# Attention inner loop: the two heads' score matmuls issued apart, with head a's value matmuls between them

## What is computed

```python
def reference(...):
    xn = _layernorm(x)
    x = x + attn(xn) + ffn(xn)
    return x

# attn
Q = rope((x @ Wq.T + bq) as 32 heads of 64)
K = rope((x @ Wk.T + bk) as 8 heads of 64), repeated 4 times
V = (x @ Wv.T + bv) as 8 heads of 64, repeated 4 times
scores = einsum('bhqd,bhkd->bhqk', Q, K) / sqrt(64)
attn = einsum('bhqk,bhkd->bhqd', softmax(scores), V)
out = attn @ Wo.T + bo

# ffn
gated = silu(x @ w_gate.T) * (x @ w_up.T)      # hidden 8192
out = gated @ w_down.T
```

## Time and profile before

| what | value |
|---|---|
| median of the 3 runs shown | 4861.9 us |
| the 3 runs | 4738.34, 4861.9, 4987.0 us |
| the profiled execution | 4735.85 us |
| its span, slowest core (core 1) | 4734.3 us |
| spans of the 8 cores | 4723.9 to 4734.3 us |
| busy: TensorE, ScalarE, VectorE | 3513.7, 1321.4, 902.3 us |

### The profile page before, as it was taken

How to read it: one execution, slowest core, us unless ns; L and a number is a source line. 1 busy time by engine, 2 the same in 40 slices (tenths; PEclk the granted TensorE clock), 3 DMA queues, 4 the chain that set the end, 5 groups by cost and what they waited for, 6 DMA issues and landing times.

```text
span 4734.3 us, 36748 instructions; the slowest of 8 cores (4723.9 to 4734.3 us)
## 1 busy us (share of the span) xinstructions
PE 3513.7 (74%) x13898; PEld 1223.7 (26%) x13898; DVE 902.3 (19%) x1009; ACT 1321.4 (28%) x1612; POOL 224.2 (5%) x428
## 2 busy tenths in 40 slices
PE   3656555555777777777777777749998995999899
PEld 0212111111211111111111111114444442444344
DVE  3242333333011111111111111130000002000000
ACT  1010111111555555555555555500000000000000
POOL 0000000000000000000000000001110000111000
PEclk9868766666988888888888888869999997999999
DMA  5242433333000000000000000059998886998887
GB/s 103 42 89 47 79 82 83 80 80 80 0 0 1 0 0 0 0 0 0 1 0 0 0 0 0 0 104 152 153 150 156 166 167 126 153 153 151 157 167 146
DMA packets 95338, 340.09 MB, mean 72 GB/s; under 512 B 10784, under 2 KB 10816, under 8 KB 90688
## 3 DMA queue, kind: packets, MB, share of 16 engines
q0 software_dynamic: 60608, 274.81, 34.0%
q1 hardware_dynamic: 34560, 62.93, 4.6%
HBM read 604.07 MB, written 8.39 MB: 129 GB/s over the span
## 4 chain that ended last, share of the span: by engine, by line
PE 47%; ACT 23%; DMA 12%; DVE 12%; issue 4%; DVEq 0%; POOL 0%; ACTq 0%; SPq 0%; POOLq 0%
ACT pta L453 11%; ACT ptb L453 10%; PE pb L611 9%; PE pb L601 9%; PE pb L438 7%; DMA wo_sb<-wo_t 6%; PE pb L293 6%; PE pb L648 5%; DMA xf_sb<-x_t 3%; PE pb L345 3%; DVE rz_sb L506 2%; DVE rz_sb L508 2%; PE pb L643 2%; DMA xf<-x_t 1%; DVE scrf L271 1%
## 5 line engine op out<-in xcount | busy, mean ns | idle before, releaser
L453 ACT ACTIVATE pta<-pb,negb_sb 128x1024 bf16<-128x1024 f32 x512 | 570.1, 1113 | 779.4 <-PE pb L438 779.3
L453 ACT ACTIVATE ptb<-pb,negb_sb 128x1024 bf16<-128x1024 f32 x512 | 566.4, 1106 | 0.0
L601 PE MATMUL pb<-xt,wg_sb 128*128 128x512 bf16 x2048 | 474.2, 383 | 95.4 <-DVE xt L582 95.4
L438 PE MATMUL pb<-qt_all,kt_all 64*128 64x512 bf16 x2048 | 328.2, 396 | 283.5 <-ACT ptb L453 282.9
L611 PE MATMUL pb<-xt,wu_sb 128*128 128x512 bf16 x2048 | 467.0, 382 | 0.0
L648 PE MATMUL pb<-gated,wd_sb 128*128 128x512 bf16 x2048 | 447.3, 379 | 0.0
L480 PE MATMUL pb<-ptb,v_all 128*64 128x512 bf16 x1024 | 420.1, 410 | 0.8 <-DVE pb L421 0.4
L617 ACT ACTIVATE silu_sb<-pb 128x512 bf16<-128x512 f32 x128 | 76.4, 597 | 1172.6 <-PE pb L601 1172.6
L487 PE MATMUL pb<-ptb,ones_bf 128*1 128x512 bf16 x1024 | 391.7, 382 | 0.0
L506 DVE RECIPROCAL rz_sb<-pb 1x1024 f32<-1x1024 f32 x16 | 104.8, 6551 | 1491.5 <-PE pb L487 1491.5
L293 PE MATMUL pb<-xt_sb,wk_sb 128*128 128x512 bf16 x512 | 206.5, 536 | 206.3 <-DVE xt_sb L274 206.3
(11 more groups left out here) (98 smaller groups left out, 1904.6 us busy)
## 6 DMA issues: line engine op xcount, KB each, us to landing
wg_sb<-wg_t POOLq DMA_DIRECT2D x128, 512.0 KB, 5.7
wu_sb<-wu_t POOLq DMA_DIRECT2D x128, 512.0 KB, 5.7
wd_sb<-wd_t POOLq DMA_DIRECT2D x32, 2048.0 KB, 14.7
xf_sb<-x_t SPq DMA_DIRECT2D x128, 256.0 KB, 2.6
xt_sb<-x_t POOLq DMA_DIRECT2D x32, 512.0 KB, 13.0
wk_sb<-wk_t POOLq DMA_DIRECT2D x32, 512.0 KB, 6.3
wq_sb<-wq_t POOLq DMA_DIRECT2D x32, 512.0 KB, 5.2
wo_sb<-wo_t POOLq DMA_DIRECT2D x32, 512.0 KB, 18.6
```

What stands on the lines that cost most here:

```text
L438: last = em.emit("tensor", (lambda p, j, c, h, base, ps: lambda t: t.matmul(ps[:, 512 * h:512 * (h + 1)], kt_all[base:base + 64, 4096 * p ...
L453: "scalar", (lambda par, ps, pt: lambda s: s.activation(pt[:, TOK * par:TOK * (par + 1)], ps[:, :], AF.Exp, bias=negb_sb[:, :], scale=0.12 ...
L601: mg = em.emit("tensor", (lambda par, dc: lambda t: t.matmul(pg[par][:, :], wg_sb[:, 2048 * par + 128 * dc:2048 * par + 128 * (dc + 1)], x ...
```

## The change

`S_quad(c)` is replaced by `S_head(c, hh)`, which issues the two score matmuls of one head, waits only for that head's exponential of the chunk before, and has a mark of its own for ScalarE to wait on. At the first chunk of a pair it waits for that head's last exponential of the pair before. The loop issues head a's scores, then head a's value matmuls of the chunk before, then head b's scores, then head b's value matmuls. Number and shape of all instructions stay the same.

```diff
-        def S_quad(c):
-            w_s = [a_ready, a_ready_sc, negb_tok, exp_a.get(c - 1), exp_b.get(c - 1)]
+        def S_head(c, hh):
+            base = 64 * hh
+            ps = psa if hh == 0 else psb_
+            ex = exp_a if hh == 0 else exp_b
+            w_s = [a_ready, a_ready_sc, negb_tok, ex.get(c - 1)]
             if j > 0 and c == 0:
-                w_s += list(prev_pair_exp)
+                w_s.append(prev_pair_exp[hh])
             last = None
             for h in range(2):
-                for hh in range(2):
...
-                        waits=(w_s if (h == 0 and hh == 0) else []),
-                        inc=(S_PE if (h == 1 and hh == 1) else None))
-            s_a[c] = s_b[c] = last
+                last = em.emit("tensor", (lambda p, j, c, h, base, ps: lambda t: t.matmul(
...
+                    waits=(w_s if h == 0 else []),
+                    inc=(S_PE if h == 1 else None))
+            (s_a if hh == 0 else s_b)[c] = last
...
         for c in range(NKCH):
-            S_quad(c)
+            S_head(c, 0)
             EXP(c, 0)
+            if c >= 1:
+                AV(c - 1, 0)
+            S_head(c, 1)
             EXP(c, 1)
             if c >= 1:
-                AV(c - 1, 0)
                 AV(c - 1, 1)
```

More of the change, by code:

```diff
@@ L427, in build_nc @@
         s_b = {}
-        def S_quad(c):
-            w_s = [a_ready, a_ready_sc, negb_tok, exp_a.get(c - 1), exp_b.get(c - 1)]
+        def S_head(c, hh):
[3 more added lines that the diff above has]
+            w_s = [a_ready, a_ready_sc, negb_tok, ex.get(c - 1)]
             if j > 0 and c == 0:
-                w_s += list(prev_pair_exp)
+                w_s.append(prev_pair_exp[hh])
             last = None
             for h in range(2):
-                for hh in range(2):
[L436 to L442, removed]
-                        waits=(w_s if (h == 0 and hh == 0) else []),
-                        inc=(S_PE if (h == 1 and hh == 1) else None))
-            s_a[c] = s_b[c] = last
+                last = em.emit("tensor", (lambda p, j, c, h, base, ps: lambda t: t.matmul(
+                    ps[:, 512 * h:512 * (h + 1)],
+                    kt_all[base:base + 64, 4096 * p + 128 * c:4096 * p + 128 * (c + 1)],
+                    qt_all[base:base + 64, TOK * j + 512 * h:TOK * j + 512 * (h + 1)],
+                    start=True, stop=True))(p, j, c, h, base, ps),
+                    waits=(w_s if h == 0 else []),
+                    inc=(S_PE if h == 1 else None))
+            (s_a if hh == 0 else s_b)[c] = last
         def EXP(c, hh):
```

## The result

The changed kernel is slower by a fifth: 5837.8 us (median of 10 runs, 5775.05 to 5967.87) against 4831.7 us (median of 10 runs of the kernel before, 4738.34 to 4987.0). The ratio is 1.215, with a 95% interval from 1.207 to 1.223. The profiled execution took 5788.5 us, 1052.7 more than that of before.

What follows compares the result with a forecast made beforehand. The prediction took the wait for both exponentials, 2.967 us a chunk, as the bound; TensorE at 2.88 would replace it. Gains of 2.5 and 0.05 less 0.51 give 2.1 us a pair, 33 in all: 4703 us, range 4640 to 4865.

Steps and rivals of the forecast that it cites:

- first two terms: Steady chunks: waits removed would allow roughly 2.1 us, but TensorE's work rises from 2.37 to 2.88, against 2.967 before.
- The ring: In each chunk, scores wait for both exponentials, 2.96 us; split by head, each ring is 1.95 us.
- the price of the unpaired scores: In each chunk, each head's two score matmuls issued alone take 0.52 us, where four paired took 0.53.
- a change of kind: Step between score and value matmuls on TensorE: 0.09 us over a matmul's 0.22; four a chunk instead of two.
- Rival 3: Added changes of kind in each chunk drain the array: chunk 3.22 us, 126 us slower, 4862 us; chance 0.07.
- third term: Ends of a head pair: at the low-clock start chunk 2 begins as before, at about 2051.5; the end costs 0.51 us more.
- rival 5: At a pair's start the clock rises some 3.4 us earlier: 21 us spared, 4682 us; chance 0.82 together with the forecast.
- the sum: Over the attention pairs: 28 x 0.09 plus 0.05 less 0.51 gives 2.1 us a pair, 33 us for sixteen.
- Rival 4: TensorE without gaps in attention is granted a tenth less clock: 0.24 us more a chunk, 108 us, 4811 us; chance 0.05.

Runs made afterwards that it cites:

- f1: Changed kernel with chunks 0 to 2 of each pair in the order of before, the rest with heads apart; ratio 0.9953 to before.
- e1: Changed kernel with each score matmul on all 128 rows instead of its head's 64; 4614.3 us against 4755.6 for before.
- g1: Changed kernel with every matmul of a chunk, scores and values of both heads, on rows 0 to 63 alone; 5675.8 us.
- e2: Changed kernel with chunks 0 to 7 of each pair in the order of before; median 4990.1 us, cores 0 to 3 of the profiled execution end at 4712.
- n1: Changed kernel for chunks 0 to 15 of each pair, the order of before for chunks 16 to 31; 5230.3 us.
- e4: Changed kernel's scores, exponentials and value matmuls grouped by query half instead of by head, each score group holding both heads; 4614.6 and 4623.3 us.
- m1: Kernel of e4 with the column of ones widened to 64 columns as in e5; ratio 0.906 to before, 4307 to 4313 us.
- e5b: Kernel before with the column of ones widened from 1 to 64 columns and nothing else; 4736.4 us.
- f2: Changed kernel with score matmuls on all 128 rows in chunks 0 to 3 of each pair alone; 4706.3 us against 4755.8 for before.
- e5: Changed kernel with the weights of the ones matmul widened from 1 to 64 columns, and its zeroing from 1 to 64 partitions; 5201.9 us.
- k1: Changed kernel plus 64 unused 128 x 128 x 512 matmuls on TensorE at each pair's end, during the reciprocals; 5775.7 us.
- e3: Kernel before with its four score matmuls in the order a, a, b, b instead of a, b, a, b; 4775.3 us against 4755.6.

## Why the prediction was wrong

The first two terms held. The ring opened: TensorE's waits for the exponentials are gone. TensorE became the bound, and the price of the unpaired scores was right: 2.88 us a chunk were forecast, f1 shows 2.91 at the clock on which the forecast rested. The value taken for a change of kind (0.09 us) held within 0.02, and e1 shows 0.22, without it, between scores and head a's values when both use 128 rows. The Trainium skill, "TensorEngine Tiling (Array Packing)", Key Properties, calls it a drain at a change of mode; e1 and g1 agree that it hangs on the tile and not on the change of weights: it went where the rows became equal, and stayed (0.52 in e1, 0.99 in g1 at the low clock) where the step is to 64-column values. The measured 0.09 is its size at the full clock. Rival 3, a full drain, did not come true.

What failed is the third term, the start of a pair. It took the clock's rise at the place where the kernel before has it, and rival 5 even moved it forward, "because TensorE is busier from 2046.3 on". TensorE was busier, and the clock did not rise in the pair at all, so the 28 steady chunks, which the sum takes at 1.00, ran at 0.50. The low clock was no longer confined to some 8 us of each pair but held through all of it, and that cost 16 x 30 x 2.11 = 1013 us. The Trainium skill, "TensorE: Matmul & The Clock Gate", in its table of goals, says that keeping TensorE continuously busy brings the full clock; 157 of 160 us busy at 0.50 disagree, and the measurement decides.

Rival 4 had the right effect under a wrong argument. I weighed it by the feed-forward stage, where TensorE is busy without a gap at 1.00, as if the busy share of the view were what counts. But those matmuls use all 128 rows. It was priced at a tenth off the clock, while the earlier trace rows show it at 1.00 or at 0.50: it had to be priced at 1.2 GHz, which the earlier trace rows would have given as 0.98 + 1.06 + 0.98 + 2.13 = 5.15 us a chunk and some 5780 us in all, against 5788.5 measured. Every number was in the text; the case was not worked out.

What the runs show of the cause, and what they leave open:

- The clock rises and stays if two heads' scores share the array (before, e2, f1, n1, e4, m1, e5b), or if the scores use all 128 rows (e1, f2).
- It doesn't rise with lone 64-row scores, whether the ones matmul is narrow (the changed kernel), wide (e5), or everything is on 64 rows (g1).
- It isn't the number of changes between kinds (e4 has as many and rises, g1 has fewer and doesn't), and not the busy share (22.44 of 40 us at 1.00 in e5b, 40 of 40 at 0.50 in the changed kernel).
- Once up, it stays with lone 64-row scores (e2, f2, f1). The loss is a trap at the low clock. Fifteen pairs enter it through the reciprocals, the first one through the pause behind the projections, and the way out was one to three chunks in the old order (n1: at most 4.0 us; f1: three chunks).
- Open: what measure of the array's use decides; the runs tell patterns apart and take no fine steps between them. A high clock at a pair's first scores doesn't save the changed kernel as it stands (k1, and its own first pair); whether it would without the wait in chunk 0 wasn't tried.

## What to carry to other kernels

Before an order of matmuls is changed, write its cost at both levels of the clock, and ask at which level each stretch starts: a pattern that would hold the high clock may be unable to reach it. A matmul on half of the rows counts as busy in every view, so a reordering that separates two of them can lose the clock while the busy share goes up. If two small groups can share the array, group the work so that each group holds both (halves of the queries here, not heads): it opened both rings, kept the clock, and with the ones on the other half of the columns gave 9.4%.

## What the runs showed of the hardware that was not expected

- The same sequence of matmuls ran at 5.08 us a chunk at 1.2 GHz and 2.91 at 2.4 GHz, to the end of a pair, depending only on the order of the three chunks ahead of it (f1).
- A 64-column and a one-column matmul on different columns follow each other by 0.33 us; two of 64 columns start together (0.00 to 0.01 apart in e5 and m1). 63 more columns of weights made the pair cheaper.
- Four score matmuls issued a, a, b, b take the 0.54 us of the order a, b, a, b (e3).
- In m1 an exponential's own row grew from 1.11 to 1.29 us, while two of them still start 1.00 apart.
- A step between 128 x 128 and 128 x 65 weights adds nothing to the 0.22 us of a matmul (e1). Between 64 and 128 rows it adds about 0.09, and so does the step from 128 columns to 64 on equal rows (e1: 0.52 instead of 0.43 for two matmuls and the step).
- In 16 of 120 pairs of k1 the filler's 1.00 was still granted at the pair's first scores, and was gone 1.0 to 1.3 us later, while TensorE waited.
